# Opening of a two-layer graph network kernel reordered: x's remainders kept in PSUM, edges asked for four pairs ahead, rows looked up behind other groups' edges, keys turned one step earlier

## Reference

```python
edge_index = jnp.stack([src, dst])             # 206250 edges, 6250 nodes, dst sorted
h = jnp.maximum(_layernorm(x, axis=-1), 0.0)   # x: 6250 x 64
x = x + _L0_gnn_ref(h, edge_index, ...)        # two gin_conv: agg = segment_sum(x[src], dst); MLP of x + agg
h = jnp.maximum(_layernorm(x, axis=-1), 0.0)
x = x + _L1_gnn_ref(h, edge_index, ...)        # segment_sum(mlp3(h[src]), dst), then mlp3(concat(h, z))
```

## Time and profile before

| | us |
|---|---|
| median of 3 runs | 959.27 (958.85 to 959.53) |
| the profiled execution | 960.25 |
| its span, first to last instruction | 958.0 |
| busy in the span: TensorE, VectorE, ScalarE, GpSimd | 883.7, 716.7, 496.7, 345.8 |
| mean granted TensorE clock | 0.99 |

### The profile page before, as it was taken

The page is one execution under the profiler, slowest core; times in us unless marked ns, Lnnn a source line. Parts: engine busy times, 40 slices in busy tenths (PEclk is TensorE's granted clock), DMA queues, the critical chain, the costliest instruction groups (busy, mean ns, idle before and its releaser), DMA issues.

```text
span 958.0 us, 25402 instructions
## 1 busy us (share of the span) xinstructions
PE 883.7 (92%) x11397; PEld 740.0 (77%) x11397; DVE 716.7 (75%) x679; ACT 496.7 (52%) x534; POOL 345.8 (36%) x255
## 2 busy tenths in 40 slices
PE   0589999999999979989999999999999989999995
PEld 0368888889989969867888887778888867777774
DVE  6879999999999979295667656665656566777672
ACT  2655555464645534264443454443444467777772
POOL 5775674638471640112567645471000000000000
PEclk9999999999999989999999999999999999999998
DMA  3024334433443333415333434434342357777761
GB/s 108 18 80 148 109 120 145 149 126 102 145 149 129 107 117 111 139 40 154 117 115 116 121 111 118 131 116 129 105 116 75 114 174 238 240 238 242 255 196 38
DMA packets 81377, 126.87 MB, mean 132 GB/s; under 512 B 9808, under 2 KB 58064, under 8 KB 81136
## 3 DMA queue, kind: packets, MB, share of 16 engines
q1 hardware_dynamic: 78128, 121.98, 40.8%
q0 software_dynamic: 3136, 3.22, 1.5%
HBM read 84.22 MB, written 40.94 MB: 131 GB/s over the span
## 4 chain that ended last, share of the span: by engine, by line
PE 50%; DVE 5%; issue 2%; ACT 1%; POOL 0%; DVEq 0%; ACTq 0%
PE net_ps_hi L1164 14%; PE net_ps_hi L1147 13%; PE net_ps_lo L1147 13%; PE net_ps_mt L1090 5%; PE net_ps_ft L1090 3%; DVE hT L849 1%; DVE hT L844 1%; PE net_ps_mt L1199 1%; ACT net_wide L1002 1%; DVE net_wide L752 1%; DVE net_first L856 1%; PE net_ps_mt L1194 1%; DVE net_h_parts L920 0%; DVE hT L909 0%; POOL net_wide L798 0%
## 5 line engine op out<-in xcount | busy, mean ns | idle before, releaser
L1002 ACT ACTIVATE net_wide<-net_raw 128x3584 fp32r<-128x3584 uint8 (+1 forms) x77 | 232.6, 3020 | 37.3 <-PE net_ps_hi L1164 25.5
L752 DVE CAST net_wide<-net_raw 128x3584 fp32r<-128x3584 uint8 (+1 forms) x103 | 202.7, 1974 | 65.2 <-PE net_ps_lo L1147 45.1
L1147 PE MATMUL net_ps_hi<-net_wide,net_first 128*128 128x512 f32 (+1 forms) x637 | 248.2, 393 | 0.1
L461 ACT ACTIVATE build_cnts<-build_ps_cnt 128x980 uint16<-128x980 f32 (+4 forms) x176 | 154.3, 901 | 167.1 <-PE build_ps_cnt L551 161.9
L1147 PE MATMUL net_ps_lo<-net_wide,net_first 128*128 128x512 f32 (+1 forms) x637 | 240.6, 381 | 0.0
L571 PE MATMUL build_ps_out<-build_parts_pad,build_cnts 128*128 128x195 bf16 x2401 | 225.4, 250 | 1.0 <-issue 0.9
L342 DVE TENSOR_TENSOR build_hot_lo<-build_grid_lo,build_keys_t 128x4096 bf16<-128x4096 bf16 x100 | 224.6, 2284 | 0.0
L571 PEld LDWEIGHTS build_ps_out<-build_parts_pad,build_cnts 128*128 128x128 fp8e4 x2401 | 205.6, 98 | 5.2 <-issue 1.8
L1164 PE MATMUL net_ps_hi<-net_wide,net_second 128*128 128x512 f32 (+1 forms) x637 | 156.7, 398 | 2.9 <-DVE net_second L934 2.4
L254 POOL DMA_INDIRECT build_edges<-in_edges,build_start_i x49 | 120.6, 2462 | 100.9 <-DVE build_start_i L326 73.6
L1164 PEld LDWEIGHTS net_ps_hi<-net_wide,net_second 128*128 128x128 f32 x637 | 115.5, 190 | 39.2 <-ACT net_wide L1002 9.7
(11 more groups left out here) (158 smaller groups left out, 670.3 us busy)
## 6 DMA issues: line engine op xcount, KB each, us to landing
net_raw<-edge_counts SPq DMA_DIRECT2D x168, 448.0 KB, 3.6
edge_counts<-build_cnts SPq DMA_DIRECT2D x168, 224.0 KB
xres<-in_x SPq DMA_DIRECT2D x1, 1568.0 KB, 7.3
net_raw<-edge_counts SPq DMA_DIRECT2D x14, 112.0 KB, 2.0
out<-xres SPq DMA_DIRECT2D x12, 128.0 KB, 4.2
build_rows<-in_dst_rows,build_row_i POOLq DMA_INDIRECT x49, 3.2
build_edges<-in_edges,build_start_i POOLq DMA_INDIRECT x49, 2.9
edge_counts<-build_cnts SPq DMA_DIRECT2D x7, 112.0 KB
```

The costliest lines, as they stand in the source:

```text
L461: nc.scalar.activation(pairs[u % A_RING][:, 0:n, :, d.start // 2:d.stop // 2], ps_cnt[b % CNT_RING][:, 0:n, 0:len(d) // 2 * NW].rearrange( ...
L752: return issue(expanded[e % WIDE_RING][:, 0:n, :, :].rearrange("p w a d -> p (w a d)"), raw[e % RAW_RING][:, 0:n, :, :].rearrange("p w a d ...
L1002: expand(act, lambda to, x: nc.scalar.activation(to, x, ACT.Identity), e).then_inc(grown["act"], 1)
L1147: last = nc.tensor.matmul(ps[(b + 1) % 2][:, 0:n * P], first[:, c, lo:lo + H], expanded[e % WIDE_RING][:, 0:n, k, :], start=(c == 0), stop ...
```

## The change

- x goes into PSUM once for each piece. Part 0 is taken off, ScalarE rounds part 1 from the bank, part 1 is taken off what is left in the same bank (`take_second`), ScalarE rounds part 2. The order of these steps on both engines is written out by hand.
- `SPANS` gets a third group of four windows; the eights start at window 10, the last group has seven windows. There are eight groups as before.
- GpSimd's requests no longer wait for steps of counts. Behind the edges of group 2 come the rows of group 3; behind those of group 3 the rows of 4 and 5; behind 4 those of 6; behind 5 those of 7 (`ROWS_BEHIND`).
- Starts of a group are found four pairs ahead of its first pair (`starts_at`), and its rows compared from six pairs ahead (`compare_step`); groups 3 and 4 have places of their own: compared in pair 1 from step 1 and in pair 5, starts in pairs 2 and 6, keys in pairs 4 and 8 (`keys_at`).
- Keys are turned at step 1 of the pair before, which is now the short step of 8 nodes. Those of pairs 1 and 2 are turned together in the opening.
- In the opening: a `Sign` of one column in front of the first comparison, `find_starts(0)` between two centrings, all four `norm_squares` ahead of the first keys, the normalization ahead of the second quarter of hots, `find_starts(2)` ahead of `find_keys(1)`; and `use(0)`'s thirds go ahead of pair 1's counts instead of behind them.

The diff, cut to its core (not shown: the matching changes of signatures and waits of `gather_rows`, `compare_rows`, `copy_first_keys` and `turn_keys`, and the removed semaphore of the early rows):

```diff
 GROUPS = P // GROUP
 HOT_RING = 5
 CNT_RING = 3
-SHORT = 2
+SHORT = 1
 TURNS = [(0, 3), (3, 5), (5, 7)]
 KEY_RING = 4
-PACE = 3, 2
 A_RING = 2
 STEP = 4
-SPANS = [(0, 2), (2, 6)] + [(w, min(w + 2 * STEP, NW)) for w in range(6, NW, 2 * STEP)]
+SPANS = [(0, 2), (2, 6), (6, 10)] + [(w, min(w + 2 * STEP, NW)) for w in range(10, NW, 2 * STEP)]
 PIECE = 7
 PIECES = NW // PIECE
 BLOCKS = -(-NW // 4)
 FIRST_PAIR = [lo // 2 for lo, hi in SPANS]
+ROWS_BEHIND = {2: (3,), 3: (4, 5), 4: (6,), 5: (7,)}
 assert 4 * 512 <= NW * (P - FX) and NW <= 49 and 2 * P * NU < FAR and NW % PIECE == 0
 
 
...
     return base(u) + 1 + max(k for k in range(steps(u)) if nodes_of(u, k).start < GROUP * (q + 1))
 
 
-def turn_step(u):
-
-    return SHORT if u else None
-
-
-def gather_step(g, j):
-
-    return (base(FIRST_PAIR[g] - 4) + 4 if FIRST_PAIR[g] >= 4 else -3) + j * PACE[0] // PACE[1]
+def compare_step(g):
+
+    return {3: (1, 1), 4: (5, 0)}.get(g, (FIRST_PAIR[g] - 6, 3))
+
+
+def starts_at(g):
+
+    return {3: (2, 1), 4: (6, 1)}.get(g, (FIRST_PAIR[g] - 4, 0))
+
+
+def keys_at(g):
+
+    return {3: (4, 1), 4: (8, 1)}.get(g, (FIRST_PAIR[g] - 1, 0))
 
 
 def build(nc, sems, dram, a, xres, sums, keys, seen_sums, ident, load_rest):
...
         ps_cnt = [ph.ps(f"ps_cnt{i}", [P, 2, 512]) for i in range(CNT_RING)]
         ps_out = [ph.ps(f"ps_out{i}", [P, 2, 256]) for i in range(2)]
         ps_key = [bank[:, :, :].bitcast(BF16)[:, :, 1024 - P:1024] for bank in ps_cnt]
+        first_keys = [ps_key[2], ps_key[0], ps_cnt[0][:, :, :].bitcast(BF16)[:, :, 1024 - 2 * P:1024 - P]]
         ps_hist, ps_row = ps_out[1][:, 0, 0:NW], ps_out[1][:, 0, 64:64 + NW]
 
         consts = ph.sem("constants_ready")
...
                 pool.wait_ge(rows_known, 1)
                 gather_rows(0, *SPANS[0])
-                gather_rows(1, *SPANS[1])
+                gather_rows(1, SPANS[1][0], SPANS[1][1] - 1)
                 gather_edges(0, *SPANS[0])
+                gather_rows(1, SPANS[1][1] - 1, SPANS[1][1])
+                gather_rows(2, *SPANS[2])
+                gather_edges(1, *SPANS[1])
...
-                half = SPANS[2][0] + STEP
-                gather_rows(2, SPANS[2][0], half, early=True)
-                gather_edges(1, *SPANS[1])
-                gather_rows(2, half, SPANS[2][1])
-                gather_edges(2, *SPANS[2])
-                for t in range(base(NU)):
-                    for g in range(2, len(SPANS)):
-                        lo, hi = SPANS[g]
-                        for j in range(4 * STEP):
-                            if gather_step(g, j) != t:
-                                continue
-                            if g > 2 and j < hi - lo:
-                                pool.wait_ge(counted, t + 1)
-                                gather_edges(g, lo + j, lo + j + 1)
-                            if g + 1 < len(SPANS) and 2 * STEP <= j < 2 * STEP + SPANS[g + 1][1] - hi:
-                                pool.wait_ge(counted, t + 1)
-                                gather_rows(g + 1, hi + j - 2 * STEP, hi + j - 2 * STEP + 1)
+                for g in range(2, len(SPANS)):
+                    gather_edges(g, *SPANS[g])
+                    for later in ROWS_BEHIND.get(g, ()):
+                        gather_rows(later, *SPANS[later])
 
...
                     norm_total(q)
                 for q in range(4):
                     norm_mean(q)
-                find_starts(0)
                 for q in range(4):
                     norm_centre(q)
-                norm_squares(0)
-                norm_squares(1)
+                    if q == 1:
+                        find_starts(0)
+                for q in range(4):
+                    norm_squares(q)
                 find_keys(0)
-                norm_squares(2)
                 chunk_hots(0, 0, GROUP)
                 lane_hots(0, 0)
-                norm_squares(3)
                 find_starts(1)
-                chunk_hots(0, GROUP, GROUP)
-                lane_hots(0, 1)
                 norm_invert()
                 for q in range(PIECES):
                     norm_scale(q)
+                chunk_hots(0, GROUP, GROUP)
+                lane_hots(0, 1)
                 chunk_hots(0, 2 * GROUP, GROUP)
                 lane_hots(0, 2)
+                find_starts(2)
                 find_keys(1)
                 chunk_hots(0, 3 * GROUP, GROUP)
                 lane_hots(0, 3)
-                find_starts(2)
                 for u in range(1, NU):
                     if u > 1:
                         chunk_hots(u, 0, P)
...
                         if q == 0 and u >= 3:
                             total_pair(u - 3)
                         for g in range(2, len(SPANS)):
-                            if (u, q) == (FIRST_PAIR[g] - 1, 0):
+                            if (u, q) == keys_at(g):
                                 find_keys(g)
-                            if g >= 3 and (u, q) == (FIRST_PAIR[g] - 3, 0):
+                            if g >= 3 and (u, q) == starts_at(g):
                                 find_starts(g)
...
-                    if g == 2:
-                        act.wait_ge(rows_early if first < STEP else rows_in[g], 16 * STEP)
-                    else:
-                        act.wait_ge(rows_in[g], 16 * (hi - lo))
...
                 def copy_first(lo, hi):
                     for k in range(lo, hi):
                         copy_counts(0, k)
 
+                def round0(q):
+                    act.wait_ge(normalized, q + 1)
+                    nc.scalar.activation(parts64[:, sevenths[q], 0, 0:F], h64[:, sevenths[q], :], ACT.Identity).then_inc(part0, 1)
+
+                def round1(q):
+                    act.wait_ge(rest, q + 1)
+                    nc.scalar.activation(parts64[:, sevenths[q], 1, 0:F], left_over(q), ACT.Identity).then_inc(part1, 1)
+
+                def round2(q):
+                    act.wait_ge(rest2, q + 1)
+                    nc.scalar.activation(parts64[:, sevenths[q], 2, 0:F], left_over(q), ACT.Identity).then_inc(part2, 1)
+
                 act.wait_ge(halves_ready, 1)
+                nc.scalar.activation(scaled[:, 0, 0:1], node_half[:, 0:1], ACT.Sign)
                 compare_rows(0)
...
-                copy_first_keys(0, 2)
+                copy_first_keys(0)
                 compare_rows(1)
...
-                copy_first(0, 4)
-                for q, w in enumerate(sevenths):
-                    act.wait_ge(normalized, q + 1)
-                    nc.scalar.activation(parts64[:, w, 0, 0:F], h64[:, w, :], ACT.Identity).then_inc(part0, 1)
-                for q, w in enumerate(sevenths):
-                    act.wait_ge(rest, q + 1)
-                    nc.scalar.activation(parts64[:, w, 1, 0:F], left_over(q), ACT.Identity).then_inc(part1, 1)
-                    if q == 2:
-                        compare_rows(2, 0, STEP)
-                    if q == 4:
-                        copy_first(4, 6)
-                compare_rows(2, STEP)
-                copy_first_keys(1, 0)
-                for q, w in enumerate(sevenths):
-                    act.wait_ge(rest2, q + 1)
-                    nc.scalar.activation(parts64[:, w, 2, 0:F], left_over(PIECES + q), ACT.Identity).then_inc(part2, 1)
+                copy_first(0, 2)
+                round0(0)
+                round0(1)
+                round0(2)
+                round1(0)
+                round0(3)
+                round1(1)
+                round2(0)
+                compare_rows(2)
+                round2(1)
+                round0(4)
+                copy_first(2, 4)
+                round1(2)
+                round0(5)
+                round1(3)
+                round2(2)
+                round2(3)
+                round0(6)
+                copy_first_keys(1)
+                copy_first_keys(2)
+                round1(4)
+                copy_first(4, 6)
+                round1(5)
+                round2(4)
+                round2(5)
+                round1(6)
+                round2(6)
                 copy_first(6, steps(0))
                 for u in range(1, NU):
                     for k in range(steps(u)):
-                        if k == turn_step(u) and u + 1 < NU:
+                        if k == SHORT and 1 < u < NU - 1:
                             copy_keys(u + 1, base(u) + k)
                         copy_counts(u, k)
                         for g in range(3, len(SPANS)):
-                            if u == FIRST_PAIR[g] - 4 and k < STEP:
-                                compare_rows(g, 2 * k, 2 * k + 2)
+                            pair, at = compare_step(g)
+                            if u == pair and 0 <= k - at < STEP:
+                                compare_rows(g, 2 * (k - at), 2 * (k - at) + 2)
 
...
                     d = nodes_of(u, k)
                     if b >= CNT_RING:
                         pe.wait_ge(copied, b - CNT_RING + 1)
-                    elif b == 2:
-                        pe.wait_ge(keys_copied, 1)
```

(75 more changed lines are left out.)

16 lines of the change are left out of this document (8 added, 8 removed).

## The result

The median went from 958.85 us (956.59 to 959.53) to 964.96 us (963.83 to 969.15, five runs); the ratio is 1.0065, interval 1.004 to 1.009: slower by 0.65%, where 949.1 was forecast. The profiled execution took 963.83 us, its span 962.0. The medians of before in later comparisons lie between 957.3 and 963.0 us, so kernels of different comparisons are set side by side by their ratio to before.

The account below looks back on a forecast made before the run. VectorE was taken to bound `build`, slightly ahead of TensorE. Terms -1.6 (D_3), -11.8 (old idle), +3.6 (new idle), +0.9 (keys), -1.3 (tail) gave -10.2: 960.25 to 950.05 us profiled, 949.1 median; range 942 to 956.

Parts of the forecast that it names:

- D_3: Start of `hot_a` of pair 3 on VectorE; forecast at 80.0 us, before 81.55, a gain of 1.6.
- D_24: Start of `hot_a` of pair 24 on VectorE; forecast at 362.6 us, before 371.46.
- the 2.6 us for edges: VectorE's forecast edge waits behind D_3: 0.7 us for group 4 and 1.9 us for the last group.
- The opening: `build` up to D_3: D_1 gains 6.6 us, but GpSimd's queue takes 7.7 back in a wait of 8 to 10.
- D_1: Start of `hot_a` of pair 1 on VectorE; forecast at 45.1 us, before 51.73, bounds 42.4 and 48.
- The first rival: Requests aren't the limit in the opening: rows at 1.25 us each, D_3 at 72, time 940; chance 0.10.
- Groups 5 and 6 have over 10 us in hand.: Steady part of `build`: edges of these groups arrive over 10 us before VectorE needs them, so no wait.
- The slower rival: Each GpSimd request is held until VectorE's next reduction: some 60 us slower, 1020; chance 0.05.
- The last group's 1.9 us: Wait ahead of the last group's keys if the last two of its seven requests are held; bounds 0 and 6.5.
- The key waits, 1.0 us: VectorE's waits for turned keys from D_3 on: 1.0 us left of 5.6, as keys turn at step 1.
- Keys for seven windows and group 4's edges, 0.9 and 0.7: VectorE from D_3 on: 0.9 us more key work in the last group, 0.7 us edge wait for group 4.
- The tail: From D_24 to the end of `build`: 25.3 us forecast, 26.6 before, 24.4 at least.

Follow-up runs that it names:

- e1: The changed kernel with a one-column VectorE memset behind each `lane_hots` of pairs 13 to 19; 948.61 us, ratio 0.9905.
- e16: The changed kernel with a one-column memset on GpSimd ahead of the first request of groups 6 and 7, none on VectorE; 971.4 us, ratio 1.0085.
- e12: The kernel before the change with memsets behind `lane_hots` of pairs 19 to 21 and keys turned at step 1; 966.04 us, ratio 1.0025.
- e2: The changed kernel with keys turned at step 2, as before the change; 968.71 us, ratio 1.0106.
- e4: The changed kernel without requests for groups 3 to 7, their rows and edges loaded by SP from fixed places, fallback left out; one execution, 938.0 us.
- e10: The changed kernel with memsets in pairs 13 to 19 and group 3 compared and its starts found two steps later; 950.07 us, ratio 0.9861.
- e3: The changed kernel with x put into PSUM twice, as before the change; 966.93 us, ratio 1.0084.
- e6: The kernel before the change with memsets behind the `lane_hots` of pairs 19 to 21; 952.19 us, ratio 0.9936.
- e7: The changed kernel with memsets in pairs 13 to 19 and x put into PSUM twice; 952.33 us, ratio 0.9938.
- e17: The kernel before the change with keys turned at step 1 and memsets behind the `lane_hots` of pairs 2 to 22; 948.63 us, ratio 0.9911.
- e11: The changed kernel with memsets from pair 9 on and starts of groups 5 to 7 found three pairs ahead; 953.09 us, ratio 0.9893.
- e18: The changed kernel with memsets in pairs 2 to 19 and group 3 compared and its starts found two steps later; 955.75 us, ratio 0.9988.
- e14: The changed kernel with a one-column `tensor_tensor` instead of a memset behind each `lane_hots` of pairs 13 to 19; 954.11 us, ratio 0.9879.
- e8: The changed kernel with memsets in pairs 13 to 20 and starts of groups 5 to 7 found three pairs ahead; 961.02 us, ratio 1.0011.

## Why the prediction was wrong

The forecast was the time without held requests, and that time is right: e1, where they are gone, measures 948.6 against 949.1. That it fits to half a microsecond is partly luck: in e1 D_3 is 1.5 us early and D_3 to D_24 takes 1.2 us longer than forecast (283.8), with 4.8 us of key waits for the forecast 1.0 and none of the 2.6 us for edges. Step by step:

- *The opening.* Right in its course. D_1 is 2.3 us later than forecast (VectorE stood 6.5 us up to there, 3.1 for the keys of pair 1 and the rest in waits of about 1), but D_3 hangs on GpSimd's queue as worked out: `find_starts(3)` at 74.26 (75.5) behind a wait of 5.1 us (8 to 10), D_3 1.3 us earlier than forecast. ScalarE waits 3.75 us for the rows, up to 68.43. The first rival (D_3 at 72) is refuted: rows at 2.5 us each did set the end. The Trainium skill ("SBUF — State Buffer", Who interferes with whom) infers that `tensor_tensor` does not stall the writing of descriptors; in the runs requests beside it take 1.9 to 3.1 us and, in the held state, 12.4, so the inference doesn't hold for these requests. The same section has an instruction with two SBUF inputs contend with GpSimd's reads and not with its writes; the 0.10 us of GpSimd's memset in e16 agree with the second half, and no run here tests the first by itself.
- *"Groups 5 and 6 have over 10 us in hand."* This is the step that failed. For group 6 eight requests at 2.5 us would have been done near 245. Three were held for 37.5 us together and the edges were 10.4 us late instead of some 16 us early. What I had of it was a price for the last group alone, 1.9 us, because the two of the earlier trace rows were "the last on GpSimd's queue". Place in the queue has nothing to do with it: those of group 6 are requests 84 to 86 of 98. What they share with the earlier trace rows is that GpSimd had been idle (15 us; 27 before) and that VectorE's last wait lay far back (21.6 us; 34.8 before). GpSimd's idle time isn't new: before the change it idles 13.5 us ahead of groups that go free. What the change moved is VectorE's last wait, from 7.0 us ahead of a group's first request to 21.6 ahead of that of group 6. In the kernel before, the earlier turn of keys does this by itself (e12). In the changed kernel the requests are held with the later turn too (e2), which points to the new places of comparisons and starts; no run sets both back, so this part is argued and not shown.
- *The slower rival* ("each request is held until the next reduction of VectorE", chance 0.05) named the mechanism and mis-sized its extent, all requests or none. Three of 49 were enough for the sign. It should have had its price per held group: 10 us for eight windows, and TensorE's clock behind it.
- *The last group's 1.9 us.* No wait there. Group 7's first request took 7.15 us and the others 3.2 and less, where two of 12 were forecast. The first ended 0.8 us behind the start of `hot_a` at 294.62, which came some 0.08 us later behind the hots than elsewhere. The last break ahead of it was the stop of 10.4 us, 15.5 us back: that was too far to keep it free.
- *The key waits, 1.0 us.* Mis-sized: 6.1. TensorE takes 0.7 us a pair longer than without requests (e4), as carried, and the keys stay late longer than assumed. That requests cost TensorE this by themselves is not so (e12).
- *Keys for seven windows and group 4's edges, 0.9 and 0.7.* The work between D_3 and D_24 is 278.59 us against 279.0, and there is no wait for group 4 in this trace. In e10 and e3 it is 3.1 and 1.0 us, within the bounds of 0 and 5.
- *The tail.* 25.9 us against 25.3.

The sum: -1.25 (D_3), -0.4 (work), +13.2 (idle), +0.6 (tail), +2.0 (`net`, 561.9 us long against 560.0), and -0.4 (1.83 us around the span instead of 2.25) make 13.8, the 963.83 against 950.05.

What the change is worth with nothing held: e1 stands 0.3% under e6, which e7 ascribes to x's remainders in PSUM (the same 3.7 us); but the order of before reaches 0.9911 as well once its keys turn earlier and all its requests are free (e17). The lead of four pairs alone brings nothing (e11). That the new order is better than the old at its best isn't shown: e10 has the lowest ratio, 0.9861, and e18, the same with more memsets, 0.9988 on another chip.

Left open: what in the chip makes the held state, and how long VectorE has to run unbroken for it. No run here varied that length alone, but the traces bound it. Take every first request of a series behind an idle time of GpSimd of over 7.5 us, from 60 us on, in all runs but e4 and e14. With VectorE's last memset, or last wait that the profile lists, up to 7.4 us back all 52 went free. With 15.5 us or more all 14 were held. None lies between. GpSimd's idle time has to lie somewhere above 2.2 us (free in e12) and was 10.0 us in the shortest case that was held (e8).

## What to carry to other kernels

Read the duration of each indirect request by itself and not as a mean: one of over 4 us that ends 0.9 us behind a reduction was held here. In this kernel that came wherever GpSimd had idled 10 us or more and VectorE had run its long two-input instructions for 15.5 us or more without a wait. Then a memset of one column on VectorE ahead of each group of requests is a cheap guard (0.06 us each, 16 us gained); those that worked here lay 0.3 to 6.4 us ahead of the first request. An edit that takes small waits out of VectorE can lose time in this way, so price the slack of a transfer at its held duration too.
